# Causal masks of an attention stage added to the scores as four 64 by 64 quarter matmuls per diagonal tile, on one Trainium2 core

## The chip, the core and the metric

One program runs on one core of a Trainium2 chip. A core has a matrix engine (TensorE, "PE"; its weight loads are shown apart as "PEld"), a vector engine (DVE), a scalar engine (ACT), GpSimd (POOL) and a sync engine (SP) that issues transfers. Matmuls write to PSUM, which has 8 banks of 128 partitions by 512 fp32. The metric is the device time of one execution in microseconds; the kernel before takes 892.85 us (median of three runs, 888.28 to 895.38).

## The reference

Four blocks with residuals: causal attention, a mixture of experts, a scan block, and the mixture of experts again. The change touches the attention alone: 4 sequences of 512 tokens, 16 heads of 8 channels, rotary embedding, and

```python
i = jnp.arange(n)
add_mask = jnp.where(i[:, None] >= i[None, :], 0.0, NEG)      # NEG = -10000.0
scores = jnp.einsum('bhqd,bhkd->bhqk', q, k) * SCALE + add_mask
attn = jax.nn.softmax(scores, axis=-1)
out = jnp.einsum('bhqk,bhkd->bhqd', attn, v)
```

## The kernel before, in words

The attention works in 32 pairs of heads (`PAIRS`; 8 pairs for each of 4 sequences). The channels of a head stand in 48 to 50 rows of bfloat16 parts; head 0 of a pair lies in partitions 0 to 63, head 1 in 64 to 127, so that two matmuls, one for each head, can lie side by side in the upper and the lower half of TensorE's rows. Each head writes a PSUM bank of its own (`to + h`).

The scores of a pair are computed twice, in tiles of 128 queries and 128 keys:

- `scores(n, u)` (units S0, S1, S2): queries on the partitions, for the row maxima that DVE takes (`row_max`, line 1384). S0 holds the tiles of 128 and 256 keys, S1 that of 384, S2 that of 512.
- `scores_T(n, u)` (units T0, T1, T2): keys on the partitions, maximum subtracted, for the exponentials of ACT (`exps`, line 710). T0 holds 512 queries, T1 384, T2 the tiles of 256 and of 128.

So there are 8 tiles per pair that touch the diagonal, 256 in all. For each, the two main matmuls (lines 953 and 978) are followed by four mask matmuls (lines 958 and 983) that add the mask to the 128 columns of the diagonal: the mask is a product of `neg_eye` (minus the root of 10,000 on a diagonal) and a 0 or 100 triangle, both held as two halves of 64 rows (`r` = 0, 1), once in each half of the partitions. All four use 64 rows, 128 columns of weights and 128 moving columns.

The order on TensorE is written out by hand. For pair n it is: S0 and S1 of pair n+1; four transposes of the queries (line 929, `queries_with_max`); the products of the probabilities of pair n-1 with the values (line 1003, `weigh_values`, 16 weight columns each); T0 of n; S2 of n+1; T1 of n; on even n the transposes of the weighed values (line 1012, unit w); T2 of n; then, in some pairs, work for the next or the last sequence (transposes of tokens line 908, projections lines 916, 923 and 1026, transposes of all keys and queries of four pairs line 929 x16, which ACT line 733 and DVE line 1375 copy).

S, T and w units go through a ring of three slots of two banks: a unit waits until the reader of the unit three places ahead of it has given the slot back (`slot_free`). A unit tells its reader with its last matmul alone. The rest of the kernel (mixtures and scan, from about 275 us) starts when the last sequence is through the attention.

Of the kernel before, what the change touches and what calls it, by code (L numbers as in the profile page):

```python
# [14 lines left out]
P = 128  # L15
D = 128
B = 4
L = 512
# [3 lines left out]
W2 = 64  # L22
# [155 lines left out]
def hybrid_block_kernel(nc, x_in, wqkv_in, wo_in, bo_in, w1_in, b1_in, w2_in, b2_in, wg_in, gate_rows_in,  # L178
# [3 lines left out]
    with ExitStack() as ctx:  # L182
        def sb(name, shape, dt=F32):
            return ctx.enter_context(nc.sbuf_tensor(name, shape, dt))

        def sem(name):
            return ctx.enter_context(nc.semaphore(name))

        ps = ctx.enter_context(nc.psum_tensor("ps", [P, 8, 512], F32))
# [21 lines left out]
        neg_eye = sb("neg_eye", [P, 2, P], BF16)  # L211
        mask_qk = sb("mask_qk", [P, 2, P], BF16)
        mask_kq = sb("mask_kq", [P, 2, P], BF16)
# [36 lines left out]
        kT, q1T = (heads_arena[:, 4096 * i:4096 * (i + 1)].bitcast(BF16).rearrange("p (b a l) -> p b a l", b=2, a=HP)  # L250
                   for i in range(2))
        q2T = sb("q2T", [P, 2, L], BF16)
# [190 lines left out]
        def slot_of(unit):  # L443
            return TURN[unit] % RING
# [450 lines left out]
        def _(pe):  # L895
            def give(unit):
                if filled(unit) > 1:
                    pe.wait_ge(slot_free[slot_of(unit)], filled(unit) - 1)
                return bank(unit)

            def read_by(unit):
                pe.wait_ge(slot_free[slot_of(unit)], filled(unit))
# [39 lines left out]
            def scores(n, u):  # L942
                a, p = divmod(n, HP)
                to = give(("S", n, u))
                if u == 0 and p % 4 == 0:
                    read_by(("kT", a, p // 4))
                    read_by(("qT", a, p // 4))
                o = 0
                for t in MAX_UNITS[u]:
                    keys = P * (t + 1)  # L950
                    for h in range(2):
                        rows = slice(W2 * h, W2 * h + MAX_AT)
                        pe.matmul(ps[:, to + h, o:o + keys], q1T[rows, a % 2, p, t * P:(t + 1) * P],  # L953
                                  kT[rows, a % 2, p, 0:keys], start=True, stop=False)
                    for r in range(2):
                        for h in range(2):
                            rows = slice(W2 * h, W2 * h + W2)
                            mm = pe.matmul(ps[:, to + h, o + keys - P:o + keys], neg_eye[rows, r, :], mask_qk[rows, r, :],  # L958
                                           start=False, stop=(r == 1))
                    o += keys  # L960
                mm.then_inc(slot_full[slot_of(("S", n, u))], 1)

# [5 lines left out]
            def scores_T(n, u):  # L968
                a, p = divmod(n, HP)
                to = give(("T", n, u))  # L970
                if u == 0:
                    pe.wait_ge(q2T_ready, n + 1)
                o = 0
                for j in PROB_UNITS[u]:
                    size = L - P * j
                    for h in range(2):
                        rows = slice(W2 * h, W2 * h + MAX_AT + 2)
                        pe.matmul(ps[:, to + h, o:o + size], kT[rows, a % 2, p, j * P:(j + 1) * P],  # L978
                                  q2T[rows, n % 2, j * P:L], start=True, stop=False)
                    for r in range(2):  # L980
                        for h in range(2):
                            rows = slice(W2 * h, W2 * h + W2)
                            mm = pe.matmul(ps[:, to + h, o:o + P], neg_eye[rows, r, :], mask_kq[rows, r, :],  # L983
                                           start=False, stop=(r == 1))
                    o += size
                mm.then_inc(slot_full[slot_of(("T", n, u))], 1)

# [51 lines left out]
            for u in range(3):  # L1039
                scores(0, u)  # L1040
            for n in range(PAIRS):
                a, p = divmod(n, HP)
                after = n + 1 < PAIRS
                if after:
                    scores(n + 1, 0)
                    scores(n + 1, 1)
                queries_with_max(n)
                if n >= 1:
                    weigh_values(n - 1)
                scores_T(n, 0)  # L1050
                if after:
                    scores(n + 1, 2)
                scores_T(n, 1)
                if n >= 2 and n % 2 == 0:
                    weighed_T(n // 2 - 1)
                scores_T(n, 2)
                if a >= 1 and p == 1:
                    post_tokens(a - 1)
                if a >= 1 and p == 2:
                    project(a - 1)  # L1060
                if a + 1 < B:
                    if p == 0:
                        pre_tokens(a + 1)
                    if p == 1:
                        pre_queries_keys(a + 1)
                        pre_values(a + 1)
                    if p in (5, 6):
                        pre_T(a + 1, "kT", p - 5)
                        pre_T(a + 1, "qT", p - 5)
# [11 lines left out]
            def give2(unit):  # L1081
                assert AT[unit] == given[0], unit
                given[0] += 1
                if AT[unit] >= BANKS:
                    pe.wait_ge(bank_free[bank_of(unit)], count_of(unit) - 1)
                return bank_of(unit)
# [7 lines left out]
            to = give2(("wa",))  # L1094
            for c in range(2):
                mm = pe.matmul(ps[0:N, to, 0:1], a_mat[:, c, :], wdt[:, c:c + 1], start=(c == 0), stop=(c == 1))
            full(("wa",), mm)
            to = give2(("sw",))
            pe.wait_ge(wb_ready, 1)
            pe.wait_ge(late_in, 64)  # L1100
            for c in range(2):
                mm = pe.matmul(ps[:, to, 0:STEP_AT + N], win_rows[:, c, :], step_inner[:, c, :], start=(c == 0), stop=(c == 1))
# [757 lines left out]
```

## Time and profile before

| | before |
|---|---|
| median of 3 runs | 892.85 us (888.28 to 895.38) |
| the profiled execution | 894.25 us |
| its span, first to last instruction | 892.4 us |
| attention, 34 to 275 us of the span | 241 us, TensorE busy 200.4 us |
| rest, 275 to 892 us | 617 us, TensorE busy 382.9 us |

The busy time of TensorE counts a matmul from its start to its modelled end; consecutive ones overlap. Where matmuls follow each other without a wait, the distance from start to start is the time that one takes on the engine. "64*128" in a matmul's row is rows by columns of its weights.

### The profile page before, as it was taken

What the parts mean: (1) busy time and instruction counts of PE and PEld (TensorE: products, weight loads), DVE (VectorE), ACT (ScalarE), POOL (GpSimd) and SP (SyncE); (2) the same over time, 40 slices, a digit from 0 to 9 for tenths busy, and PEclk for the clock granted to TensorE, in tenths of its full rate; (3) what the DMA queues carried; (4) which work ended last, traced back from release to release, by engine and by line L of the source; (5) the groups of instructions that cost most, each with busy time, mean ns of one, the idle gap of its engine ahead of it and who ended that gap; (6) DMA issues with size and microseconds to landing.
All of it is one profiled execution on the core that took longest, in us unless ns stands there. A gap on an engine that the chain in (4) does not pass through costs nothing. (4 is left out here: it accounts for less than half of the span.)

```text
span 892.4 us, 16950 instructions
## 1 busy us (share of the span) xinstructions
PE 594.1 (67%) x5836; PEld 402.2 (45%) x5836; DVE 466.1 (52%) x1241; ACT 344.4 (39%) x462; POOL 349.9 (39%) x447
## 2 busy tenths in 40 slices
PE   2588888888885635578776750567676588676730
PEld 1454445444443413466655640234354376555520
DVE  5877776776772555533222221678867543222214
ACT  1355456556652424335332320225254354332310
POOL 4152080190001575534544453114335445444550
PEclk9699999999997757789877785667687799877875
DMA  8995000000000000111110102100000111111104
GB/s 297 328 334 161 2 1 1 1 2 1 1 2 27 24 7 28 38 45 38 31 31 25 37 19 77 35 0 25 7 19 24 35 46 32 31 30 31 35 18 150
DMA packets 45146, 46.37 MB, mean 52 GB/s; under 512 B 5369, under 2 KB 42386, under 8 KB 44810
## 3 DMA queue, kind: packets, MB, share of 16 engines
q1 hardware_dynamic: 40522, 35.91, 13.5%
q0 software_dynamic: 4544, 9.38, 3.1%
q8 instruction: 52, 0.85, 0.4%
q14 instruction: 28, 0.23, 0.1%
HBM read 16.75 MB, written 28.52 MB: 51 GB/s over the span
## 5 line engine op out<-in xcount | busy, mean ns | idle before, releaser
L1650 DVE COPY arena<-ps 128x128 f32<-128x128 f32 x78 | 22.7, 292 | 211.3 <-DMA y_dram<-arena,goes_to 177.4
L831 ACT ACTIVATE arena<-ps,up_back 128x512 f32<-128x512 f32 x78 | 53.6, 687 | 194.5 <-PE ps L1194 194.5
L1194 PE MATMUL ps<-arena,w 128*128 128x128 f16 x936 | 96.6, 246 | 45.3 <-DVE arena L1636 45.0
L1384 DVE TENSOR_REDUCE row_maxima<-ps 128x2 f32<-128x256 f32 (+3 forms) x128 | 99.0, 817 | 42.8 <-PE ps L958 42.5
L710 ACT ACTIVATE probs<-ps 128x768 f32<-128x768 f32 (+1 forms) x96 | 82.5, 884 | 81.2 <-PE ps L983 81.2
L512 POOL TENSOR_TENSOR rstd<-var_eps,minus_half 128x4 f32<-128x4 f32 x16 | 17.0, 1060 | 222.6 <-DVE var_eps L1321 222.6
L1205 PE MATMUL ps<-w,probs 128*128 x936 | 95.2, 248 | 10.8 <-DVE probs L1642 10.7
L1194 PEld LDWEIGHTS ps<-arena,w 128*128 x936 | 72.2, 106 | 65.9 <-issue 55.5
L661 POOL DMA_INDIRECT y_dram<-arena,goes_to x78 | 85.0, 1090 | 34.5 <-POOL goes_to L654 20.9
L643 POOL DMA_INDIRECT rows_dram<-probs,idx x64 | 69.0, 1078 | 52.8 <-DVE idx L1582 33.0
L1205 PEld LDWEIGHTS ps<-w,probs 128*128 128x128 f16 x936 | 77.0, 111 | 21.9 <-issue 12.3
L652 POOL TENSOR_SCALAR result_row<-qk_sb,list_end 128x1 f32<-128x1 f32 x78 | 29.4, 377 | 132.0 <-DMA y_dram<-arena,goes_to 120.9
L1003 PE MATMUL ps<-probs,v_tok 128*16 128x256 f32 (+3 forms) x512 | 74.7, 434 | 2.5 <-ACT probs L710 2.5
L1642 DVE SCALAR_TENSOR_TENSOR probs<-arena,hid_scale,probs 128x512 f16<-128x512 f32 x78 | 58.2, 746 | 4.5 <-ACT probs L836 4.5
L836 ACT ACTIVATE probs<-arena,hid_scale 128x512 f16<-128x512 f32 x78 | 56.3, 721 | 2.6
L1189 PE MATMUL ps<-which,bias_rows 128*128 128x128 bf16 x312 | 37.4, 254 | 20.4 <-issue 20.0
L654 POOL TENSOR_SCALAR goes_to<-result_row,grids 128x1 int32<-128x1 f32 x78 | 46.7, 599 | 7.3
L1003 PEld LDWEIGHTS ps<-probs,v_tok 128*16 128x16 f32 x512 | 24.2, 96 | 47.7 <-issue 35.4
L953 PE MATMUL ps<-heads_arena 48*128 48x128 bf16 (+3 forms) x256 | 37.6, 308 | 11.6 <-DVE row_maxima L1384 6.4
L978 PE MATMUL ps<-q2T,heads_arena 50*128 50x512 bf16 (+3 forms) x256 | 38.5, 310 | 9.0 <-ACT probs L710 7.2
L1189 PEld LDWEIGHTS ps<-which,bias_rows 128*128 128x128 bf16 x312 | 22.1, 112 | 32.2 <-issue 31.4
L1159 PE MATMUL ps<-w,arena 128*128 128x128 f16 x384 | 26.2, 230 | 13.3 <-DVE arena L1616 8.9
(234 smaller groups left out, 1111.7 us busy)
## 6 DMA issues: line engine op xcount, KB each, us to landing
rows_dram<-grids SPq DMA_DIRECT2D x2, 8840.0 KB, 44.1
qk_sb<-rows_dram SPq DMA_DIRECT2D x78, 65.0 KB, 1.8
arena<-in_w SPq DMA_DIRECT2D x2, 2304.0 KB
arena<-y_dram SPq DMA_DIRECT2D x8, 512.0 KB, 4.0
y_dram<-arena,goes_to POOLq DMA_INDIRECT x78, 2.4
x_all<-in_x SPq DMA_DIRECT2D x4, 256.0 KB, 8.1
rows_dram<-probs,idx POOLq DMA_INDIRECT x64
out_x<-x_all SPq DMA_DIRECT2D x4, 256.0 KB, 3.7
```

The lines of the kernel that those rows point to most:

```text
L643: nc.gpsimd.indirect_dma_start(rows_dram[r].ap(), bass.IndirectOffsetOnAxis(ap=idx[:, r, b, t, k:k + 1], axis=0), xrow_words[:, b % 2, t, ...
L654: nc.gpsimd.tensor_scalar(goes_to[:, n % YT:n % YT + 1], result_row[:, n % YT:n % YT + 1], grids[:, SPARE_AT + s:SPARE_AT + s + 1], None, ...
L661: nc.gpsimd.indirect_dma_start(y_dram.ap(), bass.IndirectOffsetOnAxis(ap=goes_to[:, n % YT:n % YT + 1], axis=0), y_t[:, n % YT, :], None). ...
L710: nc.scalar.activation(probs[:, n % 2, :, PROB_AT[u]:PROB_AT[u] + size], ps[:, of:of + 2, 0:size], ACT.Exp).then_inc(slot_free[slot_of(("T ...
L831: nc.scalar.activation(hid_t[:, n % HT, :], ps[:, of, :], ACT.Gelu, scale=up_back[:]).then_inc(bank_free[of], 1)
L836: nc.scalar.activation(hid16_t[:, n % HT, 0, :], hid_t[:, n % HT, :], ACT.Identity, scale=hid_scale[:]).then_inc(high_t_ready, 1)
L1003: mm = pe.matmul(ps[quadrant:quadrant + VW, PV_BANK, j * P:L], v_tok[:, a % 2, j, 2 * p + h, :], probs[:, n % 2, h, at:at + size], start=( ...
L1189: pe.matmul(ps[:, to, c * P:(c + 1) * P], bias_rows[:, c * P:(c + 1) * P], which[:, s:s + 1].broadcast_to([P, P]), start=(c == 0), stop=Fa ...
L1194: mm = pe.matmul(ps[:, to, c * P:(c + 1) * P], w1[:, w, bass.ds(expert[s], 1), c * P:(c + 1) * P].rearrange("p o f -> p (o f)"), xgT[:, (r ...
L1205: mm = pe.matmul(ps[:, to, 0:D], hid16_t[:, n % HT, v, c * P:(c + 1) * P], w2[:, w, bass.ds(expert[s], 1), c, :].rearrange("p o d -> p (o ...
L1384: ins = nc.vector.tensor_reduce(row_maxima[:, t, 2 * p:2 * p + 2], ps[:, of:of + 2, o:o + keys], AX.X, ALU.max)
L1642: nc.vector.scalar_tensor_tensor(hid16_t[:, n % HT, 1, :], hid_t[:, n % HT, :], hid_scale[:], hid16_t[:, n % HT, 0, :], ALU.mult, ALU.subt ...
```

## The change

In both functions the four mask matmuls of a tile become four quarters. Each still uses 64 rows (`rows`, the half of the head), but 64 columns of weights (`part`, half `r` of the diagonal) and so 64 partitions of the output, and only the moving columns that this half of the output needs: for S 128 and 64, for T 64 and 128. The main matmul closes its accumulation itself (`stop=True`), and the masks add to what stands there. The number of matmuls stays.

```diff
                     for h in range(2):
                         rows = slice(W2 * h, W2 * h + MAX_AT)
                         pe.matmul(ps[:, to + h, o:o + keys], q1T[rows, a % 2, p, t * P:(t + 1) * P],
-                                  kT[rows, a % 2, p, 0:keys], start=True, stop=False)
+                                  kT[rows, a % 2, p, 0:keys], start=True, stop=True)
                     for r in range(2):
+                        part = slice(W2 * r, W2 * r + W2)
                         for h in range(2):
                             rows = slice(W2 * h, W2 * h + W2)
-                            mm = pe.matmul(ps[:, to + h, o + keys - P:o + keys], neg_eye[rows, r, :], mask_qk[rows, r, :],
-                                           start=False, stop=(r == 1))
+                            mm = pe.matmul(ps[part, to + h, o + keys - P + W2 * r:o + keys], neg_eye[rows, r, part], mask_qk[rows, r, W2 * r:],
+                                           start=False, stop=True, skip_group_check=True)
...
                     for h in range(2):
                         rows = slice(W2 * h, W2 * h + MAX_AT + 2)
                         pe.matmul(ps[:, to + h, o:o + size], kT[rows, a % 2, p, j * P:(j + 1) * P],
-                                  q2T[rows, n % 2, j * P:L], start=True, stop=False)
+                                  q2T[rows, n % 2, j * P:L], start=True, stop=True)
                     for r in range(2):
+                        part = slice(W2 * r, W2 * r + W2)
                         for h in range(2):
                             rows = slice(W2 * h, W2 * h + W2)
-                            mm = pe.matmul(ps[:, to + h, o:o + P], neg_eye[rows, r, :], mask_kq[rows, r, :],
-                                           start=False, stop=(r == 1))
+                            mm = pe.matmul(ps[part, to + h, o:o + W2 * (r + 1)], neg_eye[rows, r, part], mask_kq[rows, r, 0:W2 * (r + 1)],
+                                           start=False, stop=True, skip_group_check=True)
```

No instruction changes its place. On TensorE, the stretch from T0 to T2 of the first pairs reads, in a row, partitions by columns of the output, before:

```order
L978 MATMUL ps<-q2T,heads_arena 128x512 x2
L983 MATMUL ps<-mask_kq,neg_eye 128x128 x4
L953 MATMUL ps<-heads_arena 128x512 x2
L958 MATMUL ps<-mask_qk,neg_eye 128x128 x4
L978 MATMUL ps<-q2T,heads_arena 128x384 x2
L983 MATMUL ps<-mask_kq,neg_eye 128x128 x4
```

and with the change:

```order
L979 MATMUL ps<-q2T,heads_arena 128x512 x2
L985 MATMUL ps<-mask_kq,neg_eye 64x64 x2
L985 MATMUL ps<-mask_kq,neg_eye 64x128 x2
L953 MATMUL ps<-heads_arena 128x512 x2
L959 MATMUL ps<-mask_qk,neg_eye 64x128 x2
L959 MATMUL ps<-mask_qk,neg_eye 64x64 x2
L979 MATMUL ps<-q2T,heads_arena 128x384 x2
L985 MATMUL ps<-mask_kq,neg_eye 64x64 x2
L985 MATMUL ps<-mask_kq,neg_eye 64x128 x2
```

Before, main and mask matmuls all write 128 partitions; with the change the masks write 64 and the main ones 128, in turn.

## Rows read from the trace of the kernel before

**Rows 1.** The page: chain that ended last, shares of the span

```profile
DMA 12%; POOL 5%; issue 3%; DVE 1%; PE 1%; POOLq 0%; SPq 0%; DVEq 0%
```

**Rows 2.** Busy time by stretch: us, then each engine, PEclk, DMA share, GB/s

```profile
34.00:275.00 241.00, 200.38 (x2508) 115.35 (x2504) 172.29 (x342) 136.37 (x178) 65.11 (x87) 0.97 0.20 62
```

**Rows 3.** TensorE's waits, 40 to 290 us: total us, times, longest

```profile
PE ps L1012 <- ACT weighed L715: 14.8, 14, 1.1
PE ps L978 <- ACT probs L710: 7.2, 14, 0.5
PE ps L953 <- DVE row_maxima L1384: 5.7, 4, 2.2
PE ps L953 <- ACT heads_arena L733: 3.4, 6, 0.6
PE ps L1003 <- ACT probs L710: 2.5, 2, 1.9
PE ps L929 <- DVE q_tok L1397: 2.4, 3, 0.9
PE ps L953 <- DVE att L1406: 1.3, 3, 0.6
```

**Rows 4.** Timeline of TensorE over one pair: start us, us, operation [idle before]

```profile
221.83 0.39 PE L1003 MATMUL ps<-probs,v_tok 128*16 128x128 f32 x4
222.16 0.39 PE L978 MATMUL ps<-q2T,heads_arena 50*128 50x512 bf16 x2
222.38 0.28 PE L983 MATMUL ps<-mask_kq,neg_eye 64*128 64x128 bf16 x4
222.50 0.38 PE L953 MATMUL ps<-heads_arena 48*128 48x512 bf16 x2
...
223.78 0.28 PE L978 MATMUL ps<-q2T,heads_arena 50*128 50x256 bf16 x2 [0.51 <-ACT probs L710]
223.90 0.28 PE L983 MATMUL ps<-mask_kq,neg_eye 64*128 64x128 bf16 x4
224.02 0.22 PE L978 MATMUL ps<-q2T,heads_arena 50*128 50x128 bf16 x2
224.08 0.28 PE L983 MATMUL ps<-mask_kq,neg_eye 64*128 64x128 bf16 x4
224.31 0.23 PE L953 MATMUL ps<-heads_arena 48*128 48x128 bf16 x2
...
224.89 0.27 PE L958 MATMUL ps<-mask_qk,neg_eye 64*128 64x128 bf16 x4
225.10 0.40 PE L929 MATMUL ps<-ident,q_tok 128*128 128x128 bf16 x4
225.42 2.33 PE L1003 MATMUL ps<-probs,v_tok 128*16 128x512 f32 x16
227.69 0.39 PE L978 MATMUL ps<-q2T,heads_arena 50*128 50x512 bf16 x2
```

**Rows 5.** Timeline of ACT and of DVE over the same pair

```profile
222.70 2.50 ACT L710 ACTIVATE probs<-ps 128x1024 f32<-128x1024 f32 x3 [2.12 <-PE ps L983]
...
223.03 1.22 DVE L1384 TENSOR_REDUCE row_maxima<-ps 128x2 f32<-128x1024 f32 x1 [1.13 <-PE ps L958]
```

**Rows 6.** Timeline of TensorE where the heads' transposes of four pairs stand

```profile
216.15 1.07 PE L929 MATMUL ps<-ident,k_tok 128*128 128x128 bf16 x16
217.06 1.06 PE L929 MATMUL ps<-ident,q_tok 128*128 128x128 bf16 x16
218.05 0.23 PE L953 MATMUL ps<-heads_arena 48*128 48x128 bf16 x2
...
219.18 0.34 PE L953 MATMUL ps<-heads_arena 48*128 48x384 bf16 x2 [0.57 <-ACT heads_arena L733]
```

**Rows 7.** Weight loads by shape, 34 to 275 us: busy us, mean ns

```profile
L983 PEld LDWEIGHTS ps<-mask_kq,neg_eye 64*128 64x128 bf16 x512 | 24.7, 98 | 6.7 <-issue 0.4
L1003 PEld LDWEIGHTS ps<-probs,v_tok 128*16 128x16 f32 x496 | 23.4, 96 | 44.3 <-issue 34.3
L1026 PEld LDWEIGHTS ps<-wo,attT 128*128 128x128 f32 x24 | 2.9, 191 | 0.3
```

**Rows 8.** Timeline of TensorE at two projections, 8 matmuls each

```profile
177.30 1.89 PE L916 MATMUL ps<-wqkv,xnT 128*128 128x256 f32 x8
179.03 1.05 PE L923 MATMUL ps<-wqkv,xnT 128*128 128x128 f32 x8
```

## The prediction

> **What bounds the kernel now.** I read the chain that ended last first [rows 1]. It is made of transfers and GpSimd work of the second mixture of experts and says nothing of the attention, which is over by then. But the rest of the kernel starts only when the last sequence has left the attention, so what the attention gains or loses is gained or lost by the whole; nothing later waits for a fixed moment. The table by stretch comes next [rows 2]: the attention takes 241 us, TensorE is busy for 200.4 of them (83%), DVE for 172 and ACT for 136, and TensorE's granted clock is 0.97 of full, so at its upper level nearly throughout. TensorE comes closest to the bound but doesn't fill the stage. Its waits [rows 3] are short and of a few kinds: for the copy of the weighed values ahead of unit w (14 times, 1.1 us at most), for the first exponential ahead of T2 (14 times, 0.5 us), for the copied keys ahead of S1 (6 times, 0.6 us), and twelve more in all on maxima, probabilities, the split maximum and unit w's reader.
>
> The timeline of one pair [rows 4] shows how it closes. T0 starts at 222.16, the next T0 at 227.69: 5.53 us. Between them T0, S2 and T1 go out, and TensorE then stands for 0.51 us, since T2 needs the slots that the exponential of T0 holds; that one starts at 222.70, 0.54 us after T0 [rows 5]. After T2 (two tiles), S0 (two) and S1 (one) follow, then the transposes and the products with the values. So the loop is: T0, its exponential, T2, S0, S1, transposes, products. S2 and T1 lie beside the exponential. 15 of the 31 periods are longer, with unit w between T1 and T2, but w too waits for a copy that stands behind T0's exponential on ACT: the same tiles are on the loop.
>
> **What a mask costs now.** In [rows 4] the main matmuls of 256 columns start at 223.78, their masks at 223.90, the next main ones at 224.02: the masks hold TensorE for 0.12 us, two passes of 128 columns, each pass with both heads side by side. One pass of 128 columns is 0.057 us by the transposes (16 of them in 217.06 - 216.15 = 0.91 us [rows 6]).
>
> **What the change removes.** The four quarters use four different quarters of the array: two halves of rows (the heads) and two of columns (r). Do two halves of columns run at once? The products with the values answer that: they write 16 partitions each, the two heads in different columns of the array. The 16 of a pair cover 5120 columns, 40 times 128. The projections take (179.03 - 177.30) / 8 = 0.216 us for 256 fp32 columns, so 0.108 for 128 [rows 8]; one after another that would be 4.3 us, but they take 227.69 - 225.42 = 2.27 [rows 4]. So column parts do run side by side, and the four quarters should take one pass, 0.057 us, plus some 0.01 for four starts: 0.07 instead of 0.12, a gain of 0.05 us per tile, 13 us over 256 tiles of TensorE's time.
>
> **What the change adds.** Main matmuls have weights of 128 columns, quarters of 64. So the shape in which the array is cut changes at every step from main to mask and back. The kernel before has such changes only at a few places, and each costs:
> - masks (64*128) to transposes (128*128): 224.89 to 225.10, 0.21 us where 0.12 is usual: 0.09 [rows 4]
> - transposes to products (128*16), where rows stay and only the columns change: 0.32 us for four transposes worth 0.23: 0.09 [rows 4]
> - products back to T0: the last four, two passes worth 0.22 us, take 222.16 - 221.83 = 0.33: 0.11 [rows 4]
> - transposes to S0 (48*128): 218.05 - 217.06 = 0.99 us for 16 worth 0.91: 0.08 [rows 6]
>
> From main to mask now (both 64 or fewer rows by 128 columns) there is no such gap. I take 0.10 us for each change of shape, the same for a change of columns alone as the second one shows. The Trainium skill says the same in "TensorEngine Tiling (Array Packing)", section Key Properties: changing the tiling mode, not merely the tile, drains TensorE. It gives no time; by that rule alone the sign of the change hangs on the price, and the trace puts 0.08 to 0.11 us on it.
>
> Per tile: two changes, +0.20, less 0.05: **+0.15 us**. A tile whose masks stood ahead of a change of shape anyway (S1 ahead of the transposes, T1 ahead of w) has only one new one: +0.05. TensorE's own time grows by about 256 x 0.15 less some 62 x 0.10 (31 S1, 15 T1, 16 T2 ahead of other work), so 32 us.
>
> **How much of that reaches the end.** Along the loop of a plain pair: T0 reports after one new change less the shorter masks, +0.05; T2, two tiles, +0.30; S0, two tiles, +0.30; S1 +0.05. S2 and T1 grow inside the 0.51 us wait, which covers their +0.30 and the 0.10 by which TensorE leaves T0 later than T0 reports. Between T2 and S0 there are 0.12 us to spare (S0 waits for DVE's maximum of S2, which ends at 224.25 [rows 5] against TensorE's 224.19). DVE's maximum would come 0.20 later, TensorE 0.35, so the 0.12 are used up: 0.70 - 0.12 = 0.58 us. Half the pairs have the unit w and mostly no such slack: 0.70.
> - 16 periods x 0.58 + 15 x 0.70 = 19.8 us
> - six times the copied keys are late for S1 [rows 3, 6]: the two tiles of S0 lie in that wait, 6 x 0.30 = -1.8
> - the twelve other waits of [rows 3] (row_maxima, probs ahead of the products, q_tok, att) would take 0.30 each if what they wait for stood still; it moves in part with TensorE: half, -1.8
> - the four tiles ahead of the first pair and the end of the last: about +1
>
> Sum: 17.2 us. On the span of the profiled execution, 892.4, that is 909.6; that execution took 894.25, 1.4 above the median of the three, so against the median 892.85 it is **910 us**.
>
> **The unknown price.** No row shows weights of 64 columns in bfloat16. The nearest: loads of 128 bfloat16 columns last 98 ns, of 16 fp32 columns 96, of 128 fp32 columns 191 [rows 7]. So a load of 64 lies between nothing more and +0.09 us, and two rounds of them (r = 0 and 1 share the rows) could stand bare behind each change: +0.19. I take nothing, since the 16-column loads behind a change of shape cost nothing visible. The same page says, in Restrictions, that column tiling turns off the fast weight load; it gives no time for that here. At +0.06 per tile the loop grows by 6 x 0.06 x 31 = 11 us, to 921; at the whole 0.19 it would be about 35 us, to 945, which nothing here suggests.
>
> **Rivals.**
> 1. *No gap between shapes that keep the rows.* Then only the shorter masks are left. T0 -0.05, T2 at most -0.05 before S0 meets DVE's maximum again, S0 -0.10, S1 -0.05: some 0.25 us per pair, 8 us, **885 us**; if TensorE's whole 13 us came through, 880. For it speaks the gain by side-by-side columns, which is measured. Against it the step from transposes to products, which keeps all 128 rows and costs 0.09. It decides the other way once a change of shape costs under 0.025 us. "TensorE: Matmul & The Clock Gate", Part 3 of the Trainium skill, speaks for it: small tiles in different rows and columns run at once, and it names no price for the way in and out. Chance 0.12.
> 2. *The gaps are swallowed.* TensorE has 40 us of idle time in the stage, and if every loop were bound by DVE or ACT, 893 us would stay. Against it: between T2 and the next T0 TensorE never stands for more than 0.12 us [rows 4]. Chance 0.05.
> 3. *The gaps are larger than here,* by bare weight loads or because more standing still costs TensorE its upper clock level now and then (a pass of 128 columns takes twice as long at the lower): 918 to 930, say **922 us**. For it: weights of 64 columns have no row. Against: the granted clock is 0.97 with 17% idle time already. Chance 0.18.
> 4. My forecast, 903 to 917, **910 us**: 0.65.
>
> **How the numbers follow.** A difference of 1% is about what a measurement of this kernel can tell from none, so the bounds are 884 and 902. Slower by over 1%: forecast and rival 3, less a little of the forecast's lower end, 0.81. Within 1%: rival 2 and most of rival 1, 0.15. Faster: the fuller version of rival 1, 0.04. The range leaves out rivals 1 and 2 (0.17 between them) and the far end of rival 3: 900 to 927 us.
>
> **What would show it.** In the profile after, the start of the main matmuls of 256 columns to the start of their quarters should be 0.21 us instead of 0.12, the quarters should start within 0.02 of each other, and the next main matmuls 0.16 us later; the wait ahead of T2 should shrink from 0.51 to about 0.1; a plain period should be 6.1 us instead of 5.53, and the attention 258 us instead of 241, with the rest unchanged at 617. If the quarters start 0.12 us after the main ones and no gap follows them, my price of a change of shape is wrong and rival 1 holds. If the gaps are as said but the periods grow by less than 0.4 us, the loop is wrong.

## Result: 921 us, 3.4% slower, and the profile after

The changed kernel takes 921.4 us (median of 6 runs, 918.1 to 929.4) against 892.1 for the kernel before in the same comparison: 1.034 times as long, with a 95% interval of 1.031 to 1.037. A second measurement on another chip, told below, gives the same ratio. One execution told of below, the profiled one of after_fill, ran in a disturbed state (925.3 us where its three others took 911 to 921), so neither its time nor its clock enters a ratio or a reading. The forecast was 910 us with a range of 900 to 927: the sign, the mechanism of the gaps and the range held, the size was 17 us where it is 29. The time lies above the 903 to 917 of the likeliest case and within the range only because that had room for rival 3.

The stretches of the changed kernel (us, then the engines as in [rows 2], granted clock, DMA share, GB/s):

```profile
34.00:303.00 269.00, 245.45 (x2524) 120.58 (x2521) 166.91 (x342) 138.81 (x178) 65.13 (x87) 0.92 0.18 55
303.00:916.00 613.00, 380.48 (x3244) 274.85 (x3244) 271.21 (x844) 202.73 (x281) 271.51 (x340) 0.76 0.12 34
```

The attention ends at about 303 us instead of 275. What follows takes 613 us instead of 617; over all profiles of this study that part lies between 610 and 628 us whatever was done to the attention, so the few us by which it differs between two profiles are not put down to any edit here. The whole loss is in the attention. And there the granted clock is 0.92 instead of 0.97 [rows 2]. The clock has two levels here, full and half, so a mean of 0.92 means 2 x 0.08 x 269 = 43 us at the lower one (1.2 GHz instead of 2.4); before, it was 2 x 0.03 x 241 = 14.

A pair of heads without unit w, run at the upper level: TensorE's timeline, to be read against [rows 4]:

```profile
287.24 0.39 PE L979 MATMUL ps<-q2T,heads_arena 50*128 50x512 bf16 x2
287.56 0.25 PE L985 MATMUL ps<-mask_kq,neg_eye 64*64 64x64 bf16 x4
287.74 0.39 PE L953 MATMUL ps<-heads_arena 48*128 48x512 bf16 x2
...
288.93 0.28 PE L979 MATMUL ps<-q2T,heads_arena 50*128 50x256 bf16 x2 [0.18 <-ACT probs L710]
289.14 0.25 PE L985 MATMUL ps<-mask_kq,neg_eye 64*64 64x64 bf16 x4
289.32 0.23 PE L979 MATMUL ps<-q2T,heads_arena 50*128 50x128 bf16 x2
289.48 0.25 PE L985 MATMUL ps<-mask_kq,neg_eye 64*64 64x64 bf16 x4
289.67 0.23 PE L953 MATMUL ps<-heads_arena 48*128 48x128 bf16 x2
...
290.66 0.24 PE L959 MATMUL ps<-mask_qk,neg_eye 64*64 64x128 bf16 x4
290.83 0.40 PE L929 MATMUL ps<-ident,q_tok 128*128 128x128 bf16 x4
291.16 2.33 PE L1005 MATMUL ps<-probs,v_tok 128*16 128x512 f32 x16
293.43 0.39 PE L979 MATMUL ps<-q2T,heads_arena 50*128 50x512 bf16 x2
```

The main matmuls of 256 columns start at 288.93 and their quarters at 289.14, after 0.21 us instead of 0.12; the next main ones start 0.18 us after that instead of 0.12. The quarters do run side by side: a pass of 128 columns is 0.06 us, so the 0.18 are one pass and 0.12 of standing. Into the quarters it is 0.10, out of them 0.12, and the tile takes 0.39 us instead of 0.24. By the same reading the other tiles are 0.15 to 0.17 us longer than before, those ahead of the transposes 0.07. The pair takes 293.43 - 287.24 = 6.19 us instead of 5.53. Ahead of T2 TensorE waits 0.18 us instead of 0.51. T0 and its exponential, in another pair, stand 0.62 us apart where it was 0.54 [rows 4, 5]:

```profile
241.87 0.39 PE L979 MATMUL ps<-q2T,heads_arena 50*128 50x512 bf16 x2
...
242.49 1.75 ACT L710 ACTIVATE probs<-ps 128x1024 f32<-128x1024 f32 x2 [2.19 <-PE ps L985]
...
249.60 0.39 PE L979 MATMUL ps<-q2T,heads_arena 50*128 50x512 bf16 x2
```

That pair takes 249.60 - 241.87 = 7.73 us, not 6.19, and the difference is clock. From 245.5 to 249 us TensorE has no wait at all and is at the lower level for 3.0 of the 3.5 us:

```profile
245.50:249.00 3.50, 3.50 (x19) 1.06 (x20) 1.97 (x4) 0.97 (x2) 0.00 (x0) 0.57 0.00 0
```

TensorE's waits in all (40 to 310 us, as [rows 3]; the five largest kinds) are shorter: TensorE has moved closer to being the bound.

```profile
PE ps L1014 <- ACT weighed L715: 10.4, 14, 0.8
PE ps L953 <- DVE row_maxima L1386: 3.2, 2, 1.7
PE ps L929 <- DVE q_tok L1399: 2.9, 4, 1.4
PE ps L979 <- ACT probs L710: 2.5, 14, 0.2
PE ps L953 <- ACT heads_arena L733: 1.4, 4, 0.3
```

Another place of the same profile shows the lower clock. These are the transposes of four pairs' keys and queries, 16 each, which take 0.91 us at the upper level [rows 6]:

```profile
234.67 1.75 PE L929 MATMUL ps<-ident,k_tok 128*128 128x128 bf16 x16
236.21 1.91 PE L929 MATMUL ps<-ident,q_tok 128*128 128x128 bf16 x16
238.06 0.29 PE L953 MATMUL ps<-heads_arena 48*128 48x128 bf16 x2
```

and the stretch 236 to 238 us, with TensorE working without a break:

```profile
236.00:238.00 2.00, 2.00 (x20) 1.86 (x18) 0.00 (x0) 1.54 (x1) 0.00 (x0) 0.50 0.03 8
```

They take 1.54 and 1.85 us. Through the 44 us before this place, full of changes of shape, TensorE was at the upper level, with no wait longer than 0.74 us; the level fell at 234.9 us, just as the dense work began.

### The profile page after: what moved, and what is told of

Its sections match the earlier page's. It is cut to its first block and busy times, and to the rows that moved or that the text cites. A ratio compares the mean times of both kernels' runs of the same rounds, so it can differ in the third digit from the quotient of the medians.

```text
span 916.9 us, 16950 instructions
## 1 busy us (share of the span) xinstructions
PE 637.3 (70%) x5836; PEld 405.3 (44%) x5836; DVE 460.1 (50%) x1241; ACT 345.9 (38%) x462; POOL 348.6 (38%) x447
## 5 line engine op out<-in xcount | busy, mean ns | idle before, releaser
L1005 PE MATMUL ps<-probs,v_tok 128*16 128x256 f32 (+3 forms) x512 | 85.3, 479 | 2.0 <-ACT probs L710 2.0
L953 PE MATMUL ps<-heads_arena 48*128 48x128 bf16 (+3 forms) x256 | 41.4, 320 | 5.3 <-DVE row_maxima L1386 3.4
L979 PE MATMUL ps<-q2T,heads_arena 50*128 50x512 bf16 (+3 forms) x256 | 40.4, 312 | 4.2 <-ACT probs L710 2.5
L1184 PE MATMUL ps<-ident_f,qk_sb 128*128 128x128 f16 x156 | 25.9, 256 | 11.1 <-DMA qk_sb<-rows_dram 11.1
```

What stands on the lines that cost most here:

```text
L1005: mm = pe.matmul(ps[quadrant:quadrant + VW, PV_BANK, j * P:L], v_tok[:, a % 2, j, 2 * p + h, :], probs[:, n % 2, h, at:at + size], start=( ...
```

## Experiments

The theory after the result, to be tested: (a) each change between weights of 128 and of 64 columns costs 0.10 to 0.12 us, which lengthens the loop of a pair as forecast, some 17 us in all; (b) the other 10 to 12 us are clock: TensorE works less densely, and loses its upper level for longer. Rivals: the cost belongs to the loading of weights of 64 columns; every gap is paid in full, wherever it stands; the clock is chance, or comes with any longer loop.

**One shape for masks and main matmuls (all64).** From the changed kernel:

```diff
-                        pe.matmul(ps[:, to + h, o:o + keys], q1T[rows, a % 2, p, t * P:(t + 1) * P],
-                                  kT[rows, a % 2, p, 0:keys], start=True, stop=True)
+                        for r in range(2):
+                            at = t * P + W2 * r
+                            pe.matmul(ps[W2 * r:W2 * r + W2, to + h, o:o + keys], q1T[rows, a % 2, p, at:at + W2],
+                                      kT[rows, a % 2, p, 0:keys], start=True, stop=True)
```

and the same in `scores_T`.

> The quarters stay as in the changed kernel, and the main matmuls are cut into the same shape, 64 rows by 64 columns of weights (four for a tile instead of two, on the four quarters of the array), so that no change of shape is left between main and mask. Theory (the cost is the change of shape, 0.10 us from main to mask and 0.12 us back in the trace of the changed kernel): the gaps vanish, main and masks of a tile of 256 columns take 0.11 + 0.06 us, a plain pair about 5.3 us, and the time is 885 us (880 to 890), below the kernel before. Rival (the cost is that of loading weights of 64 columns, which stand bare): the gaps stay, and since the main matmuls get such loads too the time is 921 us or more.

Measured: 892.2 us against 891.0, ratio 1.000 (0.997 to 1.004). TensorE's timeline of it:

```profile
208.05 0.30 PE L983 MATMUL ps<-q2T,heads_arena 50*64 50x256 bf16 x4 [0.64 <-ACT probs L710]
208.19 0.23 PE L989 MATMUL ps<-mask_kq,neg_eye 64*64 64x64 bf16 x4
208.22 0.25 PE L983 MATMUL ps<-q2T,heads_arena 50*64 50x128 bf16 x4
```

The 29 us are gone, and with them every gap between main and mask: the tile of 256 columns takes 208.22 - 208.05 = 0.17 us (0.24 before, 0.39 changed), one pass of 0.06 for the masks. All weights of the tiles have 64 columns here, and a tile has eight loads of them where the changed kernel has four, so the cost is neither that of such loads nor that of more instructions. It is the change of shape. The total of 885 that I expected did not come; why is taken up below.

**The quarters of a unit together (grouped).** In S0 and T2 the two main pairs first, then both sets of quarters (and the second main matmul of a unit has `start=False`):

```diff
-                                  kT[rows, a % 2, p, 0:keys], start=True, stop=True)
+                                  kT[rows, a % 2, p, 0:keys], start=(o == 0), stop=True, skip_group_check=True)
+                    o += keys
+                o = 0
+                for t in MAX_UNITS[u]:
+                    keys = P * (t + 1)
                     for r in range(2):
```

> As the changed kernel, but in units of two tiles (S0 and T2) the main matmuls of both tiles come first and then the quarters of both. Theory (each change of shape costs 0.10 to 0.12 us): S0 and T2 each lose one pair of changes, 0.44 us per pair of heads on the loop, so a plain pair takes 5.75 us instead of 6.19 and the time falls by 14 us and by some of what the lower clock costs: 902 us (898 to 908). Rival (each set of quarters costs the same wherever it stands, by its weight loads): 921 us as the changed kernel.

Measured: 910.0 us against 891.0, ratio 1.022 (1.016 to 1.027), so about 11 us less than the changed kernel. Its timeline:

```profile
245.43 0.34 PE L983 MATMUL ps<-q2T,heads_arena 50*128 50x256 bf16 x4
245.70 0.31 PE L993 MATMUL ps<-mask_kq,neg_eye 64*64 64x64 bf16 x8
245.94 0.34 PE L953 MATMUL ps<-heads_arena 48*128 48x128 bf16 x4
```

Two tiles now take 0.51 us instead of 0.74 (288.93 to 289.67 above): one pair of changes less, 0.23 us. The direction and the price per change are right. The total missed my 902 (898 to 908): a pair without w takes 5.94 us and not 5.75. Where S0 follows T2 directly TensorE has only 0.07 us in hand there, since DVE's maximum of S2 is then due (in the changed kernel it ends at 243.00 + 1.23 = 244.23 us, S0 starts at 244.30); what T2 gives back beyond that is lost in a wait. The granted clock of its attention is 0.93. Pairs with w fell by 0.45, from 7.31 to 6.86, where 0.44 was expected.

**Quarters only beside the exponential (covered), and only on the loop (loop_only).** From the changed kernel, for S with the chosen units (2,) and then (0, 1), for T with (1,) and then (0, 2):

```diff
-                        part = slice(W2 * r, W2 * r + W2)
+                        part = slice(W2 * r, W2 * r + W2) if u in (2,) else slice(0, P)
```

with whole masks of 128 columns elsewhere.

> The kernel before, with quarters only in S2 and T1, the two units of a pair that lie beside the first exponential: 64 tiles of 256. Theory (the loop decides what is paid): the 0.33 us that they add are swallowed by the 0.51 us wait ahead of T2, but for up to 0.1 us where DVE's maximum of S2 comes too late for S0: 895 us (892 to 898). Rival (every gap is paid in full): 64 x 0.17 us, 903 us or more.

Measured: 893.4 us against 891.0, ratio 1.002 (0.999 to 1.005).

```profile
226.50 0.38 PE L953 MATMUL ps<-heads_arena 48*128 48x512 bf16 x2
226.81 0.24 PE L960 MATMUL ps<-mask_qk,neg_eye 64*64 64x128 bf16 x4
226.98 0.34 PE L980 MATMUL ps<-q2T,heads_arena 50*128 50x384 bf16 x2
227.25 0.25 PE L987 MATMUL ps<-mask_kq,neg_eye 64*64 64x64 bf16 x4
227.78 0.28 PE L980 MATMUL ps<-q2T,heads_arena 50*128 50x256 bf16 x2 [0.28 <-ACT probs L710]
```

The gaps are there (0.31 us from the main matmuls of 512 columns to their quarters, where 0.22 was usual [rows 4]), the wait ahead of T2 shrinks from 0.51 to 0.28 and swallows them; a pair takes 231.76 - 226.15 = 5.61 us (T0 to T0), 0.08 more than before. The gaps of all 64 tiles paid in full would have been 11 us, 1.2%.

> Quarters in S0, S1, T0 and T2, the units on the loop of a pair, and whole masks as before in S2 and T1, so 192 tiles of 256: the other half of the split whose first half (S2 and T1 alone) left the time at 893. Theory: these carry the whole cost of the change, a plain pair takes 6.1 to 6.2 us, the time is 916 us (911 to 921), the few us below the changed kernel being clock. Rival (each changed tile costs alike): three quarters of 30 us, 913; this run tells them apart only together with the first half.

Measured, on another chip: 920.8 us against 896.6, ratio 1.027 (1.023 to 1.031). With 0.2% for S2 and T1 alone (itself not told from nothing) this adds up to 2.9% of the 3.4%: the units on the loop carry the change. Its pairs without w take 6.19 us, as in the changed kernel, and its attention has the same clock, 0.92. 192 tiles of 256 at equal prices would have been 2.6%, inside the interval, so this run alone would not have told the two apart; the one before it does.

**Only the shorter columns (trim128).** From the changed kernel, weights and output of all 128 columns again, the moving columns cut:

```diff
-ps[part, to + h, o + keys - P + W2 * r:o + keys], neg_eye[rows, r, part], mask_qk[rows, r, W2 * r:]
+ps[:, to + h, o + keys - P + W2 * r:o + keys], neg_eye[rows, r, :], mask_qk[rows, r, W2 * r:]
```

> Weights of all 128 columns as in the kernel before, and only the moving columns cut as in the changed kernel (128 and 64 instead of 128 and 128). Theory: no change of shape, so no gap; each tile is shorter by half a pass, 0.027 us, five of them on the loop of a pair, so 4 us less: 888 us (885 to 892). Rival (the half and the full pass cost the same, because starts of matmuls or weight loads of 128 columns set the pace): 892 us.

Measured: 891.2 us against 891.0, ratio 0.999 (0.996 to 1.001): nothing to be told from no change.

```profile
225.10 0.28 PE L979 MATMUL ps<-q2T,heads_arena 50*128 50x256 bf16 x2 [0.56 <-ACT probs L710]
225.22 0.25 PE L985 MATMUL ps<-mask_kq,neg_eye 64*128 64x64 bf16 x4
225.31 0.22 PE L979 MATMUL ps<-q2T,heads_arena 50*128 50x128 bf16 x2
```

The masks take 0.09 us instead of 0.12 and a pair 228.95 - 223.51 = 5.44 instead of 5.53; 31 times that is 2.8 us, and the clock of its attention was 0.96 instead of 0.97. So the expected gain is there in the pairs and not in the total, which alone would have spoken for the rival. What the run does rule out is that the cut columns or the new `stop` flags cost the 29 us: it has both and no loss.

**The loop lengthened by work instead of standing (busy_loop).** The kernel before, whole masks, with

```diff
+                        cols = P if u == 1 else 3 * P
+                        pe.matmul(ps[:, to + h, o:o + cols], q1T[rows, a % 2, p, t * P:(t + 1) * P],
+                                  kT[rows, a % 2, p, 0:cols], start=True, stop=True)
```

ahead of the main matmuls of S, and the like ahead of those of T (128 columns in T0, 384 in T1 and T2).

> The kernel before, with whole masks of 128 columns of weights and no change of shape, but with an additional matmul ahead of each main one that lengthens TensorE's loop as the gaps of the changed kernel do: 384 moving columns (0.16 us) in the tiles of S0, S2, T1 and T2 and 128 (0.055 us) in S1 and T0; what they write is overwritten by the main matmul. So the loop is as long as in the changed kernel, but TensorE works in the time in which it stands there. Theory (a third of the loss comes from the clock, and standing in the gaps is what costs it): plain pairs take 6.15 us at the upper level, the stretches at the lower level in the attention sum to 30 us or less, as in the kernel before, and the time is 1.8 to 2.1% above the kernel before, 910 us where that takes 893. Rival (any longer loop brings the lower clock, or the clock is chance): 3.2 to 3.5% above, as the changed kernel.

> The changed kernel itself, on the chip of this call, beside the run with the loop filled by work. Both theories: 3.2 to 3.6% above the kernel before. The sum of the stretches at the lower clock in the attention was 54 us in its first profile; theory: 40 us or more again; rival (chance): anywhere from 20.

Measured, both on one chip beside the kernel before at 897.7: busy_loop 914.9 us, ratio 1.017 (1.013 to 1.021); the changed kernel again 926.7 us, ratio 1.034 (1.030 to 1.038). The attention of busy_loop and of the changed kernel's second profile:

```profile
34.00:288.00 254.00, 230.86 (x3086) 137.49 (x3084) 167.21 (x342) 136.96 (x178) 65.36 (x87) 0.99 0.19 59
```

```profile
34.00:304.00 270.00, 245.11 (x2528) 120.33 (x2526) 168.00 (x342) 138.64 (x178) 64.56 (x87) 0.92 0.18 55
```

and two T0 of busy_loop (the first matmul of each is the added one):

```profile
230.43 0.23 PE L984 MATMUL ps<-q2T,heads_arena 50*128 50x128 bf16 x2
...
236.59 0.23 PE L984 MATMUL ps<-q2T,heads_arena 50*128 50x128 bf16 x2
```

Its pairs are as long as the changed kernel's (6.16 us against 6.19, with w 7.28 against 7.31), but its clock is 0.99 and its attention 16 us shorter, 254 against 270. So a loop of this length without the standing costs 1.7%, a little less than the 1.8 to 2.1% expected, and the changed kernel pays as much again. The changed kernel's second profile has the clock of the first: 42 us at the lower level in the attention after 44. (The 54 us of the expectation also counted 10 us at the lower level before 34 us; the second profile has 52 by that count.)

The starts of T0 show where the time goes, pair by pair. Of the 31 distances from one T0 to the next, 22 ran at the upper level in busy_loop and in the changed kernel's first profile; in sum they differ by 0.1 us (each by less than 0.1, but for one of 0.5 right behind a stretch at the lower level). All of the remaining 13.9 us lie in the nine distances of which the changed kernel spent a part at the lower level. One of them is the pair of 7.73 us shown in the section on the result: it took 6.16 in busy_loop (the two T0 above are the same pair), and 6.19 in the changed kernel's second profile, where it ran at the upper level. That is the split of the loss: half of it the loop, half of it the clock. It is not chance, and not a matter of how long the loop is. What makes the level fall at one place and not at another is not shown; only that in the attention it fell nine and eight times in the changed kernel's two profiles, where TensorE stands in the gaps, and twice in busy_loop's, where it works in the same time.

**More work in the waits (after_fill, before_fill, all64_fill).** They repeat the main matmuls of T1 alone (before_fill also takes over the `stop` flags of the changed kernel in T, which cost nothing in trim128); `again` is 1 in after_fill and 2 in the other two, twice that in pairs with w:

```diff
-                    for h in range(2):
+                    for h in (0, 1) * (1 + again):
```

> The changed kernel, with the main matmuls of T1 run once more before they count (twice more in pairs with unit w), which adds 0.16 us (0.32) of matmul in a place where TensorE stands for 0.18 us (0.8) anyway; the values stay the same. Theory (the changed kernel loses some 10 us because standing longer costs TensorE its upper clock level: granted clock 0.92 in its attention against 0.97 before): more work in the gap brings the level back in part, the clock in the attention rises to 0.94 or more, plain pairs stay at 6.2 us, and the time is 914 us (910 to 918). Rival (the low stretches have nothing to do with how much TensorE works): clock 0.92 and 921 to 923 us.

Measured: 910.9, 911.6 and 921.4 us against 896.6, ratio 1.021 (1.015 to 1.027), below the changed kernel's 1.034 with its interval (which was taken on other chips). By the ratio it is 12 us faster than the changed kernel, somewhat more than expected (914 of 892 is 1.025). Adding matmuls whose results are thrown away makes the changed kernel faster. That it does so by the clock, as the theory has it, is not shown: its one profile is of the execution left out above.

> The kernel before with T1's main matmuls run twice more (four times more in pairs with unit w), 0.32 us in a wait of 0.51 (0.64 us in 1.08). Both theories: the loop stays at 5.53 us. If work in the gaps keeps the upper clock level, there is a little to win even here, since low stretches already cost a pair now and then (10.3 us where 8.7 is usual): 889 us (887 to 891). Rival (no link): 891 to 893 us.

Measured: 902.3 us against 896.6, ratio 1.006 (1.003 to 1.009): slower, which neither account expected. The pairs are as long as before (5.53 and 6.58 us), its clock 0.96 where the kernel before has 0.97. Its attention is 4 us longer, and by the starts of T0 all of that lies in four of the 31 distances, the ones with a part at the lower level, which lasts 20 us in all where it was 14. So more work in the waits went with more of the lower level here, against the theory. Filling waits is no recipe by itself, and what decided it stays open.

> The kernel whose main matmuls and masks both have weights of 64 columns, with T1's main matmuls run twice more (four times more in pairs with unit w), 0.32 us in a wait of 0.64 (0.64 us in 1.2). That kernel has pairs 0.14 us shorter than before but the same total, with a granted clock of 0.94 in the attention. Theory (the clock took the gain back): the clock rises to 0.97 and the time falls to 887 us (884 to 889), below the kernel before. Rival (no link): 892 us, or a little more where the added work comes in the way.

Measured: 892.8 us against 896.6, ratio 0.996 (0.993 to 0.998), where 887 us was expected, with the clock of the attention at 0.98. A gain of this size needs a repeat.

**all64 with and without the fill, again, five rounds on one chip.**

> The kernel with main matmuls and masks both of 64 columns of weights, a second time and in more rounds: its first ratio to the kernel before was 1.000 (0.997 to 1.004). Theory (4 us won on the loop, partly taken back by the clock): 0.995 to 1.000. Rival (all of it is taken back): 1.000 to 1.003.

> The same kernel with T1's main matmuls repeated in TensorE's waits, a second time and in more rounds, on the same chip as the one without: its first ratio was 0.996 (0.993 to 0.998). Theory (the repeats hold the upper clock level): 0.993 to 0.998, and below the one without. Rival (no link): the same as the one without, within 0.002.

Measured against 897.7: without fill 896.0, ratio 0.999 (0.997 to 1.001); with fill 896.4, ratio 0.999 (0.997 to 1.002). The two are the same, though the fill again goes with a higher clock in the attention:

```profile
34.00:275.00 241.00, 193.84 (x3027) 102.99 (x3024) 171.59 (x342) 135.13 (x177) 65.21 (x87) 0.95 0.20 62
```

```profile
34.00:273.00 239.00, 205.68 (x3416) 113.34 (x3413) 172.57 (x342) 135.55 (x178) 65.19 (x87) 0.97 0.21 63
```

(the first without, the second with it). So the 2 us by which the attention is shorter don't show in the total. The 0.996 was not confirmed, and no version here is proved faster than the kernel before; all64 is its equal, with the masks at half their price.

## The prediction, point by point

- **What bounds the kernel.** Right: the loss is all in the attention, whose 28 us more are the 29 us of the whole within what the rest varies by.
- **Quarters side by side.** Right. One pass instead of two, in the changed kernel and, without gaps, in all64.
- **Price of a change of shape.** Forecast 0.10 both ways, from four other changes [rows 4, 6]; measured 0.10 into the quarters and 0.12 out. Per tile +0.15 forecast, +0.15 to 0.17 measured. The Trainium skill says in "TensorEngine Tiling (Array Packing)", Key Properties, that changing the tiling mode, not just the tile, drains TensorE. The trace agrees as far as the 0.10 to 0.12 us of standing at each change go, and all64 agrees with the other half: going to another tile of the same shape leaves no gap.
- **The loop.** 0.58 us for a plain pair and 0.70 with w were forecast; 0.66 and 0.73 came (5.53 to 6.19, 6.58 to 7.31, in the pairs that ran at the upper level). The exponential of T0 starts 0.62 us after T0 instead of 0.54, where I had +0.05, and the gap out of T2 and S0 is 0.02 longer each. Only five of the 31 distances from T0 to T0 are plain ones of 5.53 us; in the six of 8.16 and 9.25 us, where S1 waits for the copied keys, the growth is 0.33 and 0.37, about the 0.30 less that the forecast allowed for them. The 22 distances at the upper level in both profiles grew by 11.6 us, 0.53 each; at that rate 31 of them grow by 16 us, against a forecast of 17.2 (an estimate from these starts of T0). busy_loop, whose loop is as long, agrees: 1.7% of 897.7 is 15.4 us, in a kernel that also lost 3 us less to the clock than the one before (7 us at the lower level in its attention instead of 14). Covered is in keeping with S2 and T1 being swallowed.
- **The unknown price.** Nothing was the right value for it: loads of 64 bfloat16 columns (busy us, mean ns, as [rows 7]) last 105 ns against 98, and in all64, with twice as many of them as in the changed kernel, none stands bare between main and mask.

```profile
L959 PEld LDWEIGHTS ps<-mask_qk,neg_eye 64*64 64x64 bf16 x512 | 14.7, 105 | 20.3 <-issue 14.6
```

- **The clock: the step that failed.** The sum went by a granted clock of 0.97 throughout and had no term for it; the lower level stood in rival 3 alone, as something that happens "now and then", with 922 us, which is where the time came out. The argument against it, that 17% of idle time had left the clock at 0.97, read the stage as an average. The measured term is some 14 us: 43 us at the lower level instead of 14, where each us does half the work; 13.9 us in nine of the 31 distances between busy_loop and the changed kernel's first profile; and 16 us between busy_loop and its second profile in the whole attention. So the likeliest case had the right mechanism and half of the loss; rival 3 named the missing half and its size, at a chance of 0.18.
- **Rivals 1 and 2** (no gap; gaps swallowed) are ruled out by the gaps and by loop_only.
- all64 was expected at 885 and came to 892 and 896 (of 891 and 898). Its pairs are 0.14 us shorter (5.39 and 6.45), not 0.25: after T2 it is DVE's maximum that S0 waits for, as the forecast of rival 1 had said for T2 alone, and with w S1 waits for unit w's reader. What was left went to the clock (0.95): in the second profile the 26 distances from T0 to T0 at the upper level are 4.8 us shorter in sum than in the kernel before, the other five 5.0 us longer. So rival 1 too was priced too well at 885.

## To carry to other kernels

Matmuls with fewer weight columns on separate parts of the array can pay only in runs of the same shape: each step between shapes costs 0.10 to 0.12 us here, about twice what the quarters of a tile save, and a tile has two, so either everything in the run is cut alike or nothing is. (Cut alike, the masks came at half their price here, and the total still did not move.) Count every such step on the loop that closes, not in the engine's sum: 64 tiles with such steps cost 0.2% beside a wait, and three times as many cost 2.7% on the loop. And where many short gaps are added to TensorE, allow a term for its clock: here it was about as large as the gaps themselves. What sets that term is open, so its size has to be measured.

## Of the hardware, unexpected

- The clock term. Attention profiles with gaps on the loop have granted clocks of 0.92 (changed kernel, twice), 0.92 (loop_only) and 0.93 (grouped); those without lie between 0.95 and 0.99, the highest in busy_loop, which has the longest loop of them but works through it. TensorE counted as busy for 91% of the attention in the changed kernel (245 of 269 us), 83% before, and again 91% in busy_loop (231 of 254) with its clock of 0.99: the busy time of overlapping matmuls hides the 0.1 us gaps, and does not tell what the clock will do. Nor does the longest wait: the fall at 234.9 us came after 44 us without a wait over 0.74 us.
- Useless work made a kernel faster: repeating T1's matmuls took the changed kernel from 1.034 to 1.021 times the kernel before. Twice as many repeats made the kernel before slower by 0.6%, which is unexplained.
- Four matmuls on the four 64 by 64 quarters of the array start together and cost one pass, even where two of them read the same rows of the operand (all64: 512 columns on all four quarters, then masks, in 0.27 us, 206.47 to 206.74):

```profile
206.47 0.41 PE L983 MATMUL ps<-q2T,heads_arena 50*64 50x512 bf16 x4
206.71 0.23 PE L989 MATMUL ps<-mask_kq,neg_eye 64*64 64x64 bf16 x4
206.74 0.41 PE L955 MATMUL ps<-heads_arena 48*64 48x512 bf16 x4
```
